# Attention loop of a two-layer kernel: residual update on ScalarE and GpSimd, queries turned by ScalarE, keys placed by DMA, and a new order on all engines

## What is computed

```python
xn = layer_norm(logmap0(x))
xm = expmap0(xn * (1 + sc_msa) + sh_msa)
q, k, v = [_to_heads(plin(xm, w, b)) for w, b in ...]      # 16 heads of 16
qt, kt, vt = logmap0(q), logmap0(k), logmap0(v)
attn = softmax(einsum('bhqd,bhkd->bhqk', qt, kt) / sqrt(HD))
out_h = expmap0(einsum('bhqk,bhkd->bhqd', attn, vt))
attn_out = plin(_from_heads(out_h), w_o, b_o)
attn_t = g_msa * logmap0(attn_out)
x = mobius_add(residual, expmap0(attn_t))                  # = A * residual + B * attn_t, A and B per row
```

## Time and profile before

| what | us |
|---|---|
| median of 3 runs | 1301.0 (1292.18 to 1301.76) |
| the profiled execution, its own time | 1299.24 |
| its span, first to last instruction | 1297.4 |
| TensorE busy | 1100.0 |
| VectorE busy | 1040.9 |
| ScalarE busy | 847.4 |
| GpSimd busy | 603.2 |
| first scores(0) to last scores(0) (457.69 to 973.84), 15 turns | 516.15 |

### The profile page before, as it was taken

One profiled execution on the slowest core, in us unless ns is written; L12 is line 12 of the kernel. 1 busy time (PEld: TensorE's weight loads), 2 busy tenths in 40 slices (PEclk: granted clock), 3 DMA queues, 4 the chain that ended last, 5 costly groups with the idle time before them and its releaser, 6 DMA issues.

```text
span 1297.4 us, 21034 instructions
## 1 busy us (share of the span) xinstructions
PE 1100.0 (85%) x6272; PEld 781.0 (60%) x6294; DVE 1040.9 (80%) x2502; ACT 847.4 (65%) x2246; POOL 603.2 (46%) x1059
## 2 busy tenths in 40 slices
PE   8999958774894698999999999999988678888885
PEld 7888833332342476777777777777777345555544
DVE  6887758887778467888888888888786789999984
ACT  3555468877883255666666666666655788888873
POOL 2345336654575524444334333444321356676764
PEclk9999989997897699999999999999886889999998
DMA  7334321425975343333333333333314346666633
GB/s 238 111 114 99 102 74 58 162 114 165 365 219 175 97 104 92 85 96 99 98 98 92 87 88 93 99 94 83 68 49 112 69 97 163 163 163 163 163 98 114
DMA packets 116290, 156.37 MB, mean 121 GB/s; under 512 B 9296, under 2 KB 99536, under 8 KB 114640
## 3 DMA queue, kind: packets, MB, share of 16 engines
q1 hardware_dynamic: 115632, 155.03, 43.3%
q10 hardware_dynamic: 544, 0.00, 0.0%
HBM read 111.22 MB, written 27.00 MB: 107 GB/s over the span
## 4 chain that ended last, share of the span: by engine, by line
issue 23%; POOL 15%; PE 15%; ACT 8%; DVE 7%; POOLq 0%; DMA 0%; SPq 0%; ACTq 0%; DVEq 0%
POOL t_qk L1974 4%; PE t_bk L1396 4%; POOL t_u L1904 4%; POOL t_u L1909 3%; PE t_fB L1417 2%; PE t_bk L2040 2%; PE t_fA L2054 1%; ACT t_vbd L1461 1%; ACT t_vbd L1477 1%; PE t_fB L2054 1%; ACT t_junk L1435 1%; PE t_bk L2027 1%; PE t_fA L1379 1%; ACT t_y L1524 1%; DVE t_qt L1629 1%
## 5 line engine op out<-in xcount | busy, mean ns | idle before, releaser
L1396 PE MATMUL t_bk<-k_w12g,t_ut 128*128 128x512 f32 x256 | 125.7, 615 | 2.6 <-ACT t_ut L1517 1.2
L2162 ACT ACTIVATE t_ysq<-t_y 128x768 f32<-128x768 f32 x64 | 53.6, 838 | 64.2 <-DVE t_y L2341 63.3
L412 POOL TENSOR_SCALAR s_hleak<-s_hring,k_leak 128x128 f32<-128x128 f32 x128 | 47.6, 372 | 101.4 <-ACT s_hring L367 94.3
L2054 PE MATMUL t_fA<-k_wqkv,t_ut 128*128 128x512 f32 (+1 forms) x256 | 91.5, 501 | 1.2 <-ACT t_ut L2145 1.2
L2054 PE MATMUL t_fB<-k_wqkv,t_ut 128*128 128x512 f32 (+1 forms) x256 | 90.9, 498 | 0.0
L2040 PE MATMUL t_bk<-t_vbd,t_qt 128*128 128x66 f32 x512 | 75.7, 310 | 16.3 <-DVE t_o L2356 16.3
L1915 POOL TENSOR_SCALAR t_s_su<-t_s_ru 128x4 f32<-128x4 f32 x16 | 3.8, 236 | 184.0 <-ACT t_s_ru L2153 184.0
L280 PE MATMUL s_gsum<-s_hring,k_w0t 128*128 128x128 f32 x512 | 77.9, 295 | 7.9 <-ACT s_hring L367 3.3
L2040 PEld LDWEIGHTS t_bk<-t_vbd,t_qt 128*128 128x128 f32 x512 | 70.7, 221 | 20.4 <-DVE t_o L2356 18.4
L1396 PEld LDWEIGHTS t_bk<-k_w12g,t_ut 128*128 128x128 f32 x256 | 50.4, 198 | 53.9 <-issue 49.3
L2356 DVE TENSOR_TENSOR t_o<-t_bk,t_rden 64x128 f32<-64x128 f32 x256 | 74.0, 289 | 8.5
(11 more groups left out here) (380 smaller groups left out, 3200.7 us busy)
## 6 DMA issues: line engine op xcount, KB each, us to landing
t_scb<-g_rows SPq DMA_DIRECT2D x64, 256.0 KB, 4.8
t_shb<-g_rows SPq DMA_DIRECT2D x64, 256.0 KB, 5.3
hidden_rows<-k_own SPq DMA_DIRECT2D x6, 1536.0 KB, 5.4
s_xrow<-in_x_dram SPq DMA_DIRECT2D x16, 512.0 KB, 3.6
k_hs<-s_hring SPq DMA_DIRECT2D x16, 512.0 KB, 3.1
b_xin<-in_x_dram SPq DMA_DIRECT2D x16, 512.0 KB, 4.5
x_rows<-b_xout SPq DMA_DIRECT2D x16, 512.0 KB, 5.1
t_xf<-x_rows SPq DMA_DIRECT2D x16, 512.0 KB, 4.8
```

The costliest lines, as they stand in the source:

```text
L1396: last = nc.tensor.matmul(z.fW[:, j, :], z.ut[:, c, j * P:(j + 1) * P], k["w12g"][:, c, :], start=False, stop=(c == C - 1))
L2054: last = nc.tensor.matmul(dst[:, w0:w1], ut[:, c, j * P:(j + 1) * P], k["wqkv"][:, c, w0:w1], start=(c == 0), stop=(c == C - 1))
L2162: nc.scalar.activation(ysq[:, j % 2, :], y[:, j, :], ACT.Square).then_inc(s["ysq_ready"], 1)
```

## The change

The residual update becomes a scaling of xb on ScalarE (`xs_ready`), after scaled_a, and one sum of 128x1024 on POOL behind qk, which raises `x1_ready` by 4; VectorE's moved() stays only for the last group. q is turned (copied from PSUM) by ScalarE in place of VectorE. The keys are copied once by ScalarE into kt, which lies in the memory of o, and 8 DMAs on SP place them in kpar, 16 partitions each; kpar is set to zero once at the start, and its layout changes, so that the 128 weights of a scores matmul lie 8 floats apart. The reciprocals of two neighbouring outputs are taken in one instruction. POOL sets its three tiles to zero before norm(0), VectorE splits the biases behind modulate(0). The orders of SP, POOL, PE, ACT and DVE change as shown.

```diff
-        kpar = m.sb("kpar", [P, C, GB, 2, T])
+        kpar = m.sb("kpar", [P, C, 2, GR])
-        rden = m.sb("rden", [P, 2, PAIRS // 2, 2])
+        rden = m.sb("rden", [P, 4, PAIRS // 2, 2])
+        kt = flat_o.rearrange("p (c r) -> p c r", c=C)
...
 # SP, turn(i)
-                if mid:
-                    if i >= 2:
-                        sp.wait_ge(s["x1_ready"], (i - 1) * GT)
-                    sp.dma_start(xb[:, :, :], row_group(k["x_dram"], i - 1)).then_inc(s["xb_loaded"], 16)
                 if front:
                     sp.wait_ge(s["qts_ready"], (i + 1) * C)
...
                         sp.dma_start(qbd[r, :, p, :], qt[r, :, :]).then_inc(s["qbd_loaded"], 16)
+                    sp.wait_ge(s["kt_ready"], (i + 1) * C)
+                    for p in range(4):
+                        for par in range(2):
+                            r = slice(32 * p + HD * par, 32 * p + HD * (par + 1))
+                            sp.dma_start(kpar[r, :, par, :], kt[r, :, :]).then_inc(s["kpar_loaded"], 16)
+                if mid:
+                    if i >= 2:
+                        sp.wait_ge(s["x1_ready"], (i - 1) * GT)
+                    sp.dma_start(xb[:, :, :], row_group(k["x_dram"], i - 1)).then_inc(s["xb_loaded"], 16)
...
 # POOL
-            norm(0)
-            shift(0)
-            clip_u(0)
-            for t in (vbd[:, :, :, :, :], qbd[:, :, :, :]):
+            for t in (vbd[:, :, :, :, :], qbd[:, :, :, :], kpar[:, :, :, :]):
                 start.do(pool.memset(t, 0.0))
...
             pool.wait_ge(s["zero_ready"], 1)
+            norm(0)
+            shift(0)
+            clip_u(0)
...
                 if tail:
                     scaled_norms(i - 2)
+                    gate_step(i)
                 if head:
                     shift(i + 1)
-                if tail:
-                    gate_step(i)
...
+                if tail:
+                    pool.wait_ge(s["ab_ready"], (i - 1) * GT)
+                    pool.wait_ge(s["xs_ready"], (i - 1) * GT)
+                    rows = k["x1"][:, (i - 2) * GT:(i - 1) * GT, :]
+                    pool.tensor_tensor(rows, rows, xb[:, :, :], ALU.add).then_inc(s["x1_ready"], GT)
                 if head:
                     clip_u(i + 1)
...
 # PE
-                        pe.wait_ge(s["kpar_ready"], i * (2 * C))
+                        pe.wait_ge(s["kpar_loaded"], i * (8 * 16))
...
-                                last = nc.tensor.matmul(bk[r][:, at:at + 2 * T], kpar[rows, c, e, :, :].rearrange("p a t -> p (a t)"),
+                                last = nc.tensor.matmul(bk[r][:, at:at + 2 * T], kpar[rows, c, :, :].rearrange("p a (t b) -> p (a t) b", b=GB)[:, :, e],
...
+                if head:
+                    turn_x(i + 1)
                 if mid:
                     values(GB - 2)
                     values(GB - 1)
-                if head:
-                    turn_x(i + 1)
...
 # ACT: the order before was exp 0, square 0, square 1, norms_a, exp 1, square 2, tanh_parts, exp 2, square 3,
 # inverse, roots of the head norms, exp 3, scaled_a
+ exponentials(0), square_y(0), norms_a, square_y(1), tanh_parts, exponentials(1), square_y(2), inverse,
+ exponentials(2), square_y(3), roots of the head norms, exponentials(3), scaled_a, then:
+                    for j in range(GT):
+                        nc.scalar.activation(xb[:, j, :], xb[:, j, :], ACT.Copy, scale=sc["A"][:, j:j + 1]).then_inc(s["xs_ready"], 1)
...
                 if front:
-                    for cc in range(C):
-                        act.wait_ge(s["qkt_ready"], i * (2 * C) + (C + cc + 1))
-                        for par in range(2):
-                            nc.scalar.activation(kpar[:, cc, :, par, :], by_batch(bk[C + cc][:, :]), ACT.Copy,
-                                                 scale=k["mask"][:, par:par + 1]).then_inc(s["kpar_ready"], 1)
+                    for c_ in range(C):
+                        act.wait_ge(s["qkt_ready"], i * (2 * C) + (c_ + 1))
+                        if i >= 1 and c_ == 0:
+                            act.wait_ge(s["qbd_loaded"], i * (4 * 16))
+                        nc.scalar.activation(qt[:, c_, :], bk[c_][:, :], ACT.Copy).then_inc(s["qts_ready"], 1)
+                    for c_ in range(C):
+                        act.wait_ge(s["qkt_ready"], i * (2 * C) + (C + c_ + 1))
+                        nc.scalar.activation(kt[:, c_, :].rearrange("p (t b) -> p b t", b=GB), by_batch(bk[C + c_][:, :]), ACT.Copy).then_inc(s["kt_ready"], 1)
                 if head:
                     squares_u(i + 1)
+                    norms_u(i + 1)
...
-                if head:
-                    norms_u(i + 1)
...
 # DVE
-                def output(e):
+                def outputs(e0, e1):
+                    dve.wait_ge(s["pv_ready"], (i - 1) * GB + e1)
+                    dens = bank[:, 2 + e0 % 2:2 + e0 % 2 + e1 - e0, 0:PAIRS * VW].rearrange("p e (q c w) -> p e (q c) w", c=2, w=VW)
+                    nc.vector.reciprocal(rden[:, e0 % 4:e0 % 4 + e1 - e0, :, :].rearrange("p e q c -> p e (q c)"), dens[:, :, :, 2 * HD]).then_inc(s["rden_ready"], e1 - e0)
+                    dve.wait_ge(s["rden_ready"], (i - 1) * GB + e1)
+                    for e in range(e0, e1):
+                        scaled_output(e)
...
 # DVE, turn(i): the order before was product 0, gated, product 1, head_norms 0, output 0, product 2, head_norms 1,
 # modulate, output 1, product 3, head_norms 2, output 2, head_norms 3 and total, output 3, sb and fac, outputs 4
 # and 5, moved, outputs 6 and 7, copies of q, vbd, yo, moments
+ product 0, gated, product 1, head_norms 0, outputs(0, 2), product 2, head_norms 1, modulate, product 3,
+ head_norms 2, head_norms 3 and total, outputs(2, 4), sb and fac, outputs(4, 6), outputs(6, 7), outputs(7, 8),
+ vbd, yo, moments
...
             modulate(0)
+            second.split_bias(flat_o[0:1, 0:3 * D], flat_ot[0:1, 0:3 * D // 2].bitcast(BF16))
```

More of the change, by code:

```diff
@@ L1753, in attention_mlp @@
         pt = (ptile[:, :], flat_qt)
+        kt = flat_o.rearrange("p (c r) -> p c r", c=C)
         flat_qbd = qbd[:, :, :, :].rearrange("p c q r -> p (c q r)")
-        flat_kpar = kpar[:, :, :, :, :].rearrange("p c e a t -> p (c e a t)")
+        flat_kpar = kpar[:, :, :, :].rearrange("p c a r -> p (c a r)")
         flat_vbd = vbd[:, :, :, :, :].rearrange("p j h q w -> p (j h q w)")
@@ L2206, in turn @@
                     return {"norms_a": norms_a, "tanh_parts": tanh_parts, "inverse": inverse, "scaled_a": scaled_a}
-                for e in range(GB):
-                    if mid and e in (0, 2, 3, 5):
-                        exponentials((0, 2, 3, 5).index(e))
-                    if front and e < GT:
-                        square_y(e)
-                    if i == NG and e == 3:
-                        once(second.norms_u, 0)
-                    if i == NG and e == 5:
-                        once(second.scaled_u, 0)
-                    if i == NG - 1 and e == 2:
-                        scales_a.scalar_norms(act)
-                    if i == NG - 1 and e == 5:
-                        scales_a.scalar_log(act)
-                    if i == NG - 1 and e == 7:
-                        scales_a.scalar_root(act)
-                    if tail and i <= NG and e == 1:
-                        norms_a()
-                    if tail and i <= NG and e == 2:
-                        tanh_parts()
-                    if tail and i <= NG and e == 4:
-                        inverse()
-                    if front and e == 4:
-                        act.wait_ge(s["tot_ready"], i + 1)
-                        nc.scalar.activation(rnh[:, :], hsum[:, :], ACT.Ln, bias=eps2[:, 0:1]).then_inc(s["lnh_ready"], 1)
-                        act.wait_ge(s["lnh_ready"], i + 1)
-                        nc.scalar.activation(rnh[:, :], rnh[:, :], ACT.Exp, scale=-0.5).then_inc(s["rn_ready"], 1)
-                    if tail and i <= NG and e == 6:
-                        scaled_a()
@@ new lines, in turn @@
+                if mid:
+                    exponentials(0)
+                if front:
+                    square_y(0)
+                if tail and i <= NG:
+                    norms_a()
+                if front:
+                    square_y(1)
+                if tail and i <= NG:
+                    tanh_parts()
+                if mid:
+                    exponentials(1)
+                if front:
+                    square_y(2)
+                if i == NG - 1:
+                    scales_a.scalar_norms(act)
@@ new lines, in turn @@
+                if tail and i <= NG:
+                    inverse()
+                if mid:
+                    exponentials(2)
+                if i == NG:
+                    once(second.norms_u, 0)
+                if front:
+                    square_y(3)
+                    act.wait_ge(s["tot_ready"], i + 1)
+                    nc.scalar.activation(rnh[:, :], hsum[:, :], ACT.Ln, bias=eps2[:, 0:1]).then_inc(s["lnh_ready"], 1)
```

(39 more changed lines are left out.)

8 lines of the change are left out of this document (3 added, 5 removed).

## The result

The changed kernel takes 1404.2 us (median of 4 runs, 1399.02 to 1406.36) where the kernel before, on the same chip, took 1301.38: a ratio of 1.080, 95% interval [1.073, 1.086]. The profiled execution took 1406.36 us and has a span of 1404.5. The direction was forecast, the size was not: 1348 was said, and 1404.2 is also above the range. Over the whole span VectorE is relieved as meant (80% busy before, 70% after), and yet the kernel is slower.

The account below looks back on a forecast made before the run. Each loop turn was taken as bound by TensorE and its waits for VectorE's t_o. 25.3 + 11.6 = 36.9 us a turn gave +38 over 15 turns, +47 with 3.6 + 5.2 at the start: median 1348, range 1288 to 1400.

Parts of the forecast that it names:

- Leg B: From the start of the transposes of q and k to the next scores(0): 7.87 us becomes 11.6, TensorE stalled 3.7.
- The strided weights: In scores matmuls, weights 8 floats apart cost nothing, out of a possible 0 to 4.6 us a turn.
- the rival at its upper end: In scores matmuls, strided weight loads add 1.16 us to each of 64 scores: +74, 1422 us; chance 0.16.
- Leg A without waits: From scores(0) to the transposes of q and k, without waits and at 2.4 GHz: 22.0 us, its lower end.
- The wait at values(4): TensorE waits 1.2 us there in each turn, since outputs(2, 4) now stands behind all four head norms.
- The clock: Stalls in each turn lower TensorE's granted clock, costing 1.9 us a turn, from a range of 0 to some 4.
- The last turn: The loop's last turn places no keys and was counted as unchanged.
- Sum of a turn: From one scores(0) to the next: 25.3 + 11.6 = 36.9 us, where the 15 turns took 34.4 each.
- The relief of VectorE: In the attention loop VectorE loses the update (3.42 us) and q copies (1.29); as rival paying in full 1298, chance 0.14.
- The start: Before the first products, POOL's fills ahead of norm(0) delay modulate by 3.6 us; first scores(0) waits 5.2 more for keys.
- xb behind the keys: The xb load, issued after the key DMAs, lands 2.1 us into the turn and costs nothing, with 2.5 of cover.
- The rival of the cheap issue: Key DMAs on SP are issued at 0.41 us a piece: a turn of 32.0, 1270 us in total; chance 0.13.

Follow-up runs that it names:

- a_twoq_strided: The changed kernel with its eight key DMAs shared between SP's and ScalarE's queues, strided layout and 2 KB pieces kept: 1363.23 us, ratio 1.051 to the kernel before.
- b_strided: The kernel before with only the new strided layout of the key weights, which ScalarE's masked copies write: 1344.01 us, ratio 1.035.
- a_contigdma: The changed kernel with contiguous key weights, the eight key DMAs writing pieces of 256 bytes: 1371.31 us, ratio 1.056 to the kernel before.
- a_actmask: The changed kernel with ScalarE writing the masked keys as before, no key DMAs and no fill of kpar: 1272.77 us, ratio 0.980 to the kernel before.
- m_resid: a_actmask with the residual update back on VectorE, no ScalarE scaling and no POOL sum: 1304.55 us, ratio 1.005 to the kernel before.
- m_qcopy2: a_actmask with the q copies back on VectorE, ahead of the placing of the values: 1265.68 us, ratio 0.976 to the kernel before.

## Why the prediction was wrong, point by point

- **Leg B**: right. Predicted 11.6 us with a stall of 3.7; measured 11.66 (698.15 to 709.81) and 3.72. Issues take 0.594 in the median, landings 2.4, and SP starts 2.1 after the transposes did. a_twoq_strided shows that the row of issues is the cause. ScalarE's key copies, with gaps between the elements written, did take twice as long (2.04 for two, against 1.09 for those of q) and were hidden behind the issues, as said.
- **The strided weights**: this step failed. "I take nothing, the pace of the nearest row" was wrong; the rival at its upper end, 1.16 us for each of the scores, was right but for a little: 2.17 - 1.16 = 1.0, measured alone in b_strided, and 1.1 for the scores(0) behind the stall (2.29 - 1.16). Together that is 4.15 us of a turn and 62 us of 15 turns, where the total missed by 56. Not all of it is the stride's own: scores(0) ran at a granted clock of 0.50, where contiguous scores take 2.08 (a_contigdma), so only 0.2 of its 1.1 is the stride and 0.9 is the clock. This makes 3.2 us a turn for the stride, 48 in 15 turns, the largest term of the miss. The nearest row was of the same operation and the same shape, but not of the same access, and the access was the thing that had changed. The note on cachelines in the Trainium skill, "SBUF — State Buffer", pointed the right way: b_strided shows a loss with elements 32 bytes apart, though no run here tells by which rule it grows. It had a chance of 0.16 and deserved far more.
- **Leg A without waits**, 22.0: right. 22.0 + 4.15 (stride) + 0.68 (waits for t_o) + 0.6 (products(1) 3.42 for 2.85) = 27.4, and 27.53 was measured (670.62 to 698.15).
- **The wait at values(4)**, 1.2: right in a_contigdma and a_actmask (1.02), absent in the changed kernel, since scores(3), 1.0 longer, stands between exponential 2 and values(4). The stride paid for a part of itself: taken out of the changed kernel it gives back 33 us (and some 7 more that the later landing of the small pieces takes, 0.5 in 15 turns), put into the kernel before it costs 46.
- **The clock**: 1.9 us a turn were taken. The mean turn was (1078.48 - 468.89) / 15 = 40.64 us; less 11.66, 22.0, 4.15 and 0.68 that leaves 2.15. With the 0.9 that the clock took of scores(0) it is 3.1, and a_contigdma gives the same: a mean turn of 38.95, less 12.14 for leg B and 23.7 for leg A with its waits, is 3.1. So this term was too small by 1.2 us a turn, 18 in 15 turns, though within the 0 to 4 that the prediction allowed. The kernel that the forecast had in mind, with no cost of the stride, takes 1371 us and not 1348: 18 by the clock, and 7 by the later landing of its small pieces.
- **The last turn** was taken as one like the others. It has no products(0) between the output projection and its scores(0), which waits 6.81 us for the keys. The last of the 15 turns is 45.87 us and the 14 ahead of it 40.27 in the mean, where the kernel before had 35.86 and 34.31. This is 4 us of the loss. The clock's 3.1 is a remainder and holds a part of it; by the 14 turns alone it is 2.7.
- **Sum of a turn**: predicted 36.9, measured 40.64. The difference of 3.7 is +3.2 for the stride, +1.2 for the clock and -0.7 for waits; in 15 turns 56 us, as much as the miss in the median. In the profiled execution the miss is 60 (1406.36 against 1346): 56 here, 2.4 up to the first scores(0), and the rest behind the last. Of the signs that the prediction named, the 12 issues in a row with 7.1 us from the first to the last, the stall of 3.7 us and the granted clock (0.92 over the 15 turns) came. The waits at values(4) did not, the turns are over 36 to 38 us, and scores(n) at 2.17 us is the sign that it had named for a cost of the strided loads.
- **The relief of VectorE**: right in mechanism. m_resid gives it as 2.44 us a turn from the residual update; for the copies of q m_qcopy2 shows none. The prediction named it as the cause of the waits, and a_actmask shows the kernel that it makes if nothing takes it back.
- **The start**: +3.6 predicted for the first products and +3.6 measured (428.98 to 432.59, by the first matmul of products(0)), but by luck: norm(0) took 2.17 us and not 3.44, the fills began 0.7 later, and they and the small ones took 7.85 for 7.4. The wait for the keys was 5.18 (5.2 predicted). The first scores(0) came at 468.89 (466.5): the lower clock reached further into the first products (0.6 us), and GpSimd's products of q and k took 5.95 us for 4.11; the placing of the values, no longer behind VectorE's copy of q, ran beside them (timeline of GpSimd: 451.33 to 457.28; of VectorE: 451.29 to 456.37). That collision was not seen in the prediction.
- **xb behind the keys**: right. It landed 2.4 us into the turn (2.1 predicted), VectorE's product(1) came at 676.30, 5.7 us in, and TensorE never waited for it.
- **The rival of the cheap issue** (0.41) fell with the first row of SP's queue: 0.585 at least in 128 issues.

## What to carry to other kernels

Before a layout is changed to suit a DMA, look at who else reads that tile, and how: a matmul operand that is loaded as weights once for every few columns pays the stride each time, here 1.0 us for each 16 matmuls at full clock, more than 3 us of TensorE a turn, where the copies of the keys became 0.4 us of ScalarE shorter (2.42 to 2.04). And where an operation keeps its line, shape and operands but changes its access pattern, its old duration is no forecast of the new one. When a change of many parts loses, put back the parts one by one: here the relief by the residual update was worth -2%, the path of the keys +10% on top (1404.2 against 1272.77) and the others nothing that is shown, and the wait that the good part left behind was worth another 1.5% once it was filled (1270.26 to 1250.09).
